# Attention products of a fused block as four products on 128x32 blocks of the TensorE array

## The chip, the cores and the metric

The kernel runs on one core of a Trainium2 chip. The metric is device time in microseconds, from the start of the program on the core to its end; the median of several runs is given. The profile is of one execution. PE is the matmul engine (TensorE), PEld its weight loads, DVE is VectorE, ACT is ScalarE, POOL is GpSimd and SP is the engine that issues most DMAs.

## The reference

An adaLN transformer block on x of shape (4, 2048, 256): batch 4, 2048 tokens, 256 channels. The attention has 16 heads of 16 channels, the second half of which is rotated by position.

```
h = layernorm(x) * (1 + ca) + sa
q, k, v = up-projections of h @ Wq_down, h @ Wk_down, h @ Wv_down      # 16 heads of 16
scores = q @ k.T / 4, causal mask, softmax over the keys
x = x + ga * ((att @ v) @ Wc)
h = layernorm(x) * (1 + cb) + sb
x = x + gb * moe(h)              # top 2 of 12: 8 experts of 512 hidden units, 4 that pass h on
```

## The kernel before, in words

`project` (from L254) normalises x, forms q, k and v by fp32 products on the whole 128x128 array and writes them out. q and k are split in three bf16 parts each, and six pairs of parts (L49) are stacked on the partitions, so that one bf16 product of 96 rows sums them. `attention` (from L827) follows; `route` and `experts` come after it and are not touched.

**Iterations.** The attention runs 16 times (NIT, L45): four batches by four groups of four heads. Every loop is unrolled. One iteration has two halves, and the halves of successive iterations overlap.

*Maxima.* For each tile of 128 queries and each chunk of up to 512 keys, PE multiplies queries by keys into PSUM, and DVE takes the maximum over the keys. The work is cut into 73 units (`UNITS`, L201 to L206) of two or four heads. `unit_products` (L221) issues one product of 96 rows, 128 columns of queries as weights and w keys as the moving operand, per head (L227); on the diagonal one more product per head adds the mask by way of the identity (L231). `unit_maxima` (L239) is DVE's reduction. Two PSUM buffers of two banks serve the units (NRED, L207): PE waits on `red_done` before it refills one. The first 13 units of iteration 0 are issued at the end of `project` (L677 to L680).

*The turn.* Four times per iteration DVE forms the negated maxima of 512 queries, POOL splits them in three bf16 parts (L1061), and PE turns these 48 columns into 48 rows (`turn`, L1131); DVE copies them out, and SP writes them as three more rows under the queries (L951).

*Scores, exponentials, values.* For each of 40 tiles of 128 keys by up to 512 queries (`KT`, L843), PE multiplies keys by queries once more, now with 99 rows, so that the maximum is subtracted in the product (`scores`, L1144), ACT takes the exponential from PSUM (L1192, three PSUM banks), POOL zeroes the upper triangle on diagonal tiles (L1077), and PE multiplies the values by the result (`values`, L1160). A value product is fp32, has 32 columns of weights per head, and the four heads of a tile go to four 32-partition blocks of one PSUM bank. One fp32 product is recorded as two matmuls, so a tile is a group of eight. Every other product of the attention has 128 columns of weights, the turn 48.

**The order.** `Course` (L683) is a planner that runs when the kernel is built. From costs in microseconds per operation (L686 to L688) it lays out the order in which PE takes units, turns, scores and values; POOL's and SP's orders and DVE's stream come from the same plan. A unit may run ahead of the scores by a fixed share (RUN_AHEAD). ENTER (0.09) and LEAVE (0.147) are the costs that it counts when a group of value products begins after, or is followed by, another kind of work (L717, L765, L771). Each engine then runs its list in order, and waits on semaphores.

Of the kernel before, what the change touches and what calls it, by code (L numbers as in the profile page):

```python
# [30 lines left out]
P = 128  # L31
# [12 lines left out]
NG = H // HG  # L44
NIT = B * NG  # L45
SLOT = 32
QB = 256
NJ = T // QB
COMBOS = [(0, 0), (0, 1), (1, 0), (1, 1), (0, 2), (2, 0)]  # L49
SROWS = 16 * len(COMBOS)  # L50
MROWS = 3
# [27 lines left out]
def apart(eng):  # L79

    eng.nop(nofuse=True)
# [51 lines left out]
def build(nc, a, out):  # L133
    d, retired = {}, []
    with ExitStack() as ctx:
        def dram(name, shape, dt):
            d[name] = nc.dram_tensor(name, shape, dt, kind="Internal").ap()

        dram("q_parts", (3, B, H, DH, T), BF16)
        dram("k_parts", (3, B, H, DH, T), BF16)  # L140
        dram("v_ones", (B, NG, P, TT, HG * SLOT), F32)
        dram("attn_t", (B, NG, P, T), F32)
# [69 lines left out]
def unit_view(ps, u, at):  # L212

    _, _, _, nh, w = UNITS[u]
    buf = ps[:, 4:8, :].rearrange("p (u n) w -> p u n w", u=NRED)[:, at % NRED, :, :]
    if w > 256:
        return buf[:, :, 0:w]
    return buf.rearrange("p n w -> p (n w)")[:, 0:nh * w].rearrange("p (h w) -> p h w", h=nh)


def unit_products(pe, k, ps, ks, qs, u, at):  # L221

    i, c, h0, nh, w = UNITS[u]
    o, diag = unit_view(ps, u, at), c == i // 4
    for h in range(nh):
        first = w > 256 or h % (512 // w) == 0
        ins = pe.matmul(o[:, h, :], qs[0:SROWS, h0 + h, i * P:(i + 1) * P], ks[0:SROWS, h0 + h, 512 * c:512 * c + w],  # L227
                        start=first, stop=not diag, skip_group_check=w <= 256)
    if diag:
        for h in range(nh):  # L230
            ins = pe.matmul(o[:, h, w - P:w], k["identb"][:, :], k["mask_qk"][:, :],  # L231
                            start=False, stop=True, skip_group_check=w <= 256)
    return ins


# [18 lines left out]
def project(nc, a, d, k, ps, g0, retired):  # L254
    with ExitStack() as ctx:
        def sb(name, shape, dt=F32):
            return ctx.enter_context(nc.sbuf_tensor(name, shape, dt))
# [15 lines left out]
        parts = sb("parts", [P, 2, 3, 2, NM, BLK], BF16)  # L273
        vout = sb("vout", [P, 2, TPB, H, SLOT])
        tab_ld, norm_step, std_done, hn_done, tr_done, ht_done, ones_done = (
# [36 lines left out]
        with nc.Block() as block:  # L312
# [265 lines left out]
            def _(pe):  # L578
# [98 lines left out]
                for u in range(HEAD):  # L677
                    if u >= NRED:
                        pe.wait_ge(g0["red_done"], u - NRED + 1)
                    unit_products(pe, k, ps, g0["ks"], g0["qs"], u, u).then_inc(g0["red_ready"], 1)  # L680


class Course:  # L683


    MM, MUL, MASK, ENTER, LEAVE, LATE, HOP = 1 / 2400, 0.0045, 0.0565, 0.09, 0.147, 0.1, 0.2  # L686
    TURN_PE, TURN_DVE, ROWS, ROWS_LATER, SPLIT, AFFINE, OUT, QUARTER_MAX, LOAD = 0.12, 0.3, 6.0, 10.0, 1.6, 0.65, 0.58, 0.2, 8.0
    SCALE, RUN_AHEAD, PREFER_DVE = 1.3, 0.16, 0.3  # L688

# [137 lines left out]
def attention(nc, a, d, k, ps, g0, first, retired):  # L827
    with ExitStack() as ctx:
        def sb(name, shape, dt=F32):
            return ctx.enter_context(nc.sbuf_tensor(name, shape, dt))  # L830
# [8 lines left out]
        QJ = 512  # L839
# [24 lines left out]
        for n in range(NIT):  # L864
            now, rest = [], []
            for x in ([1, 2] if n == 0 else [n + 2]):
                if x < NIT:
                    rows = [(what, x, m) for m in range(len(COMBOS)) for what in ("ks", "qs")]
# [19 lines left out]
        QUARTER = HG * KPJ  # L888
# [3 lines left out]
        ks = [g0["ks"], lent[0], sb("ks2", [P, HG, T], BF16)]  # L892
        qs = [g0["qs"], lent[1], sb("qs2", [P, HG, T], BF16)]
        num, x_in = routed_inputs(k)
        vs = sb("vs", [P, R, TT, HG * SLOT])
        probs = sb("probs", [P, NPB, HG, QJ])
# [5 lines left out]
        mparts = sb("mparts", [P, NJ, HG, MROWS, KPJ], BF16)  # L902
# [5 lines left out]
        red_ready, red_done = g0["red_ready"], g0["red_done"]  # L908
# [13 lines left out]
        def st_view(n, s):  # L922

            m, _, nh = SETS[s]
            w = QJ - KT[m][2]
            return st_ps[:, (NSET * n + s) % NST, 0:nh * w].rearrange("p (h w) -> p h w", h=nh)

        with nc.Block() as block:
            @block.sync
            def _(sp):  # L930
# [22 lines left out]
                def denominators(n):  # L953

                    for r in range(2):
                        sp.wait_ge(o_st[r], 16 * NJ // 2 * (n + 1) + 1)
                    rows = d["attn_t"][n // NG, n % NG].rearrange("(h s) (c t) -> h s c t", s=SLOT, t=HG * T // P)
                    sp.dma_start(den[:, :], rows[:, DH, :, :]).then_inc(den_ld, 16)
# [26 lines left out]
                def outputs(n, half):  # L985

                    rows = d["attn_t"][n // NG, n % NG].rearrange("(h s) t -> s h t", s=SLOT)
                    return rows[0:DH, :, half * SC:(half + 1) * SC]
# [125 lines left out]
            @block.tensor  # L1114
            def _(pe):
                def group(n, u, at):

                    r = n % R
                    if u == 0:
                        pe.wait_ge(ld[r], LD * (n // R + 1))  # L1120
                    if at >= NRED:
                        pe.wait_ge(red_done, at - NRED + 1)
                    unit_products(pe, k, ps, ks[r], qs[r], u, at).then_inc(red_ready, 1)

                def turn(n, q, at):

                    pe.wait_ge(part_step, PART * (NJ * n + q + 1))
                    pe.wait_ge(red_done, at - NRED + 1)
                    apart(pe)
                    o = red_ps[0:MROWS * QUARTER, at % NRED, 0, :].bitcast(BF16)  # L1130
                    pe.transpose(o[:, 0:P], mparts[:, q, :, :, :].rearrange("p h m i -> p (h m i)"), k["identb"][:, :]).then_inc(red_ready, 1)  # L1131

                def scores(n, r, s):

                    m, h0, nh = SETS[s]
                    J, j, lo = KT[m]
                    o = st_view(r, s)
                    if s == 0 and 0 < n < R:
                        pe.wait_ge(ones_ld, 16 * (R - 1))
                    if h0 == 0 and j == 0:  # L1140
                        pe.wait_ge(m_ld, M_LD * (NJ * n + J + 1) + 1)
                    pe.wait_ge(exp_done, NSET * n + s + 1)
                    for h in range(nh):
                        ins = pe.matmul(o[:, h, :], ks[r][0:SROWS + MROWS, h0 + h, j * P:(j + 1) * P],  # L1144
                                        qs[r][0:SROWS + MROWS, h0 + h, J * QJ + lo:(J + 1) * QJ], start=True, stop=True)
                    ins.then_inc(st_ready, 1)

                def values(n, r, m):

                    J, j, lo = KT[m]  # L1150
                    if m == 0:
                        pe.wait_ge(v_ld[r], 16 * NV * (n // R + 1))
                    if j == 0:
                        pe.wait_ge(o_done, NJ * n + J + 2)
                    if m in DIAG:
                        pe.wait_ge(mask_done, len(DIAG) * n + DIAG.index(m) + 1)
                    else:
                        pe.wait_ge(exp_done, NSET * n + of_tile[m][-1] + 1 + NST)
                    for g in range(HG):
                        ins = pe.matmul(o_ps[SLOT * g:SLOT * (g + 1), lo:QJ], vs[:, r, j, SLOT * g:SLOT * (g + 1)],  # L1160
                                        probs[:, (NKT * r + m) % NPB, g, 0:QJ - lo], start=(j == 0), stop=(m == LAST[J]))
                    ins.then_inc(pv_done, 1)

                for kind, n, x in course.pe_order:
                    if kind == "scores":
                        scores(n, n % R, x)
                    elif kind == "values":
                        values(n, n % R, x)
                    elif kind == "turn":
                        turn(n, x, unit_at[n, TURN + x])  # L1170
                    elif n > 0 or x >= HEAD:
                        group(n, x, unit_at[n, x])
                pe.wait_ge(wc_done, B)
                pe.wait_ge(first["o"][0], 16 * KC)
                pe.wait_ge(red_done, len(course.stream))
                apart(pe)
                projected(pe, k, projected_bank(ps, 0), num, 0).then_inc(first["out"][0], 1)
# [231 lines left out]
def routed_inputs(k):  # L1409

    return (k["shared"][:, 0, :].rearrange("p (x k b) -> p x k b", x=XB, k=KC),
            k["shared"][:, 1, :].rearrange("p (x j c) -> p x j c", x=XB, j=TPB))
# [9 lines left out]
def projected_bank(ps, j):  # L1422

    return ps[:, 4 + 2 * j:6 + 2 * j, :].rearrange("p n (j c) -> p (n j) c", j=2)


def projected(pe, k, o, num, t):

    for n in range(TPB):
        for c in range(KC):  # L1430
            ins = pe.matmul(o[:, n, :], num[:, t % XB, c, n * P:(n + 1) * P], k["wc"][:, t // BPS, c, :],
                            start=(c == 0), stop=(c == KC - 1))
    return ins
# [695 lines left out]
```

## Time and profile before

| | |
|---|---|
| median of 3 runs | 2607.42 us |
| lowest and highest | 2605.97 and 2611.03 us |
| span of the profiled execution, first to last instruction | 2600.7 us |
| the median less this span | 6.7 us |
| mean granted TensorE clock over the span | 0.970 of 2.4 GHz |
| busy: PE, DVE, ACT, POOL | 95%, 73%, 64%, 29% |
| matmuls and weight loads | 16056 and 16057 |

The profile gives no time of its own for the execution beside its span; the 6.7 us are what lies before the first and after the last instruction, as far as one execution can be set against the median of others. A row of a timeline reads: start, length, engine, line, operation, output<-inputs, form of the operands (weights' rows\*columns, then rows x moving columns and type), and the number of instructions merged in it; its length reaches from the start of the first to the end of the last. The starts are measured, the ends of matmuls are modelled. An idle time behind a row is the engine's own before it.

### The profile page before, as it was taken

The page shows a single profiled execution, that of the slowest core. Times are in us where ns is not written, and L with a number is a line of the kernel's source. Part 1 is how long each engine was busy: PE and PEld are TensorE (multiplying, and loading weights), DVE is VectorE, ACT ScalarE, POOL GpSimd, SP SyncE. Part 2 cuts the span into 40 slices and gives each one's busy share as a digit, 9 for nine tenths or more (in the row PEclk, how much of TensorE's full clock was granted, in tenths as well). Part 3 has the DMA queues.
Part 4 walks back from the last instruction along what each step waited for, and adds up shares of the span by engine and source line. Part 5 has one row for each costly group of instructions (what it writes and reads, how often), then busy time and mean ns, then how long its engine had stood idle before and what let it go on. Part 6 is the DMA issues. An engine that isn't in the chain of part 4 may idle for free. (4 is left out here: it accounts for less than half of the span.)

```text
span 2600.7 us, 47842 instructions
## 1 busy us (share of the span) xinstructions
PE 2470.6 (95%) x16056; PEld 1274.6 (49%) x16057; DVE 1905.6 (73%) x3219; ACT 1670.9 (64%) x2983; POOL 765.4 (29%) x894
## 2 busy tenths in 40 slices
PE   6987789999999999999999999999999889999998
PEld 3554223333333333333333333333327779899897
DVE  5887778888787887887877878878836854455665
ACT  1656347777777777777777777777775455555554
POOL 2545311111111111211111111111112657677554
PEclk8999689999999999999999999999999889999999
DMA  5698653252432433434424323231027656575665
GB/s 181 198 255 217 136 86 88 66 116 79 96 92 75 93 86 86 86 83 92 91 78 100 88 73 78 64 73 39 27 82 215 214 185 131 105 136 114 104 104 84
DMA packets 224510, 285.59 MB, mean 110 GB/s; under 512 B 29462, under 2 KB 177974, under 8 KB 223926
## 3 DMA queue, kind: packets, MB, share of 16 engines
q1 hardware_dynamic: 185308, 235.53, 35.9%
q0 software_dynamic: 31872, 41.30, 9.4%
q10 hardware_dynamic: 7136, 6.32, 0.8%
q8 instruction: 103, 1.69, 0.3%
q14 instruction: 91, 0.75, 0.1%
HBM read 143.37 MB, written 138.81 MB: 109 GB/s over the span
## 5 line engine op out<-in xcount | busy, mean ns | idle before, releaser
L239 DVE TENSOR_REDUCE mxc<-ps 128x2 f32<-128x1024 f32 (+4 forms) x1168 | 1297.7, 1149 | 314.9 <-PE ps L227 165.9
L1192 ACT ACTIVATE probs<-ps 128x512 f32<-128x512 f32 (+1 forms) x2240 | 1177.9, 587 | 461.0 <-PE ps L1144 449.2
L1160 PE MATMUL ps<-probs,vs 128*32 128x512 f32 (+3 forms) x5120 | 601.3, 542 | 1.2 <-POOL probs L1077 1.2
L1144 PE MATMUL ps<-qs,ks 99*128 99x512 bf16 (+3 forms) x1760 | 505.0, 353 | 10.6 <-DMA qs<-m_t 6.6
L227 PE MATMUL ps<-ks,qs 96*128 96x512 bf16 (+3 forms) x1760 | 465.1, 355 | 27.7 <-DVE mxc L239 18.0
L1077 POOL TENSOR_SCALAR_AFFINE_SELECT probs<-probs 128x512 f32<-128x512 f32 x256 | 162.0, 636 | 870.8 <-ACT probs L1192 870.7
L1144 PEld LDWEIGHTS ps<-qs,ks 99*128 99x128 bf16 x1760 | 147.9, 97 | 379.0 <-ACT probs L1192 270.3
L227 PEld LDWEIGHTS ps<-ks,qs 96*128 96x128 bf16 x1760 | 163.6, 99 | 181.5 <-DVE mxc L239 42.7
L1921 PE MATMUL ps<-x_t,w_at 128*128 128x128 f32 x1968 | 243.0, 277 | 0.0
L2052 POOL DMA_INDIRECT out<-ys,idx x120 | 192.6, 1605 | 138.4 <-DMA out<-ys,idx 85.1
L1921 PEld LDWEIGHTS ps<-x_t,w_at 128*128 128x128 f32 x1968 | 232.7, 194 | 0.2 <-ACT w_at L1966 0.2
L1144 PE MATMUL ps<-shared 99*128 99x512 bf16 (+3 forms) x800 | 228.4, 349 | 0.0
L1930 PE MATMUL ps<-w2t,hid_t 128*128 x960 | 227.2, 379 | 0.0
L1160 PEld LDWEIGHTS ps<-probs,vs 128*32 128x32 f32 x5120 | 101.0, 108 | 228.9 <-issue 119.1
L227 PE MATMUL ps<-shared 96*128 96x512 bf16 (+3 forms) x800 | 206.8, 348 | 2.0 <-DVE mxc L239 1.8
L1930 PEld LDWEIGHTS ps<-w2t,hid_t 128*128 128x128 f32 x960 | 173.2, 190 | 18.7
L2021 DVE TENSOR_TENSOR ys<-ps,gm 128x256 f32<-128x256 f32 x120 | 50.9, 425 | 177.4 <-PE ps L1930 127.4
L1966 ACT COPY w_at<-shared 128x1024 f32 x126 | 131.8, 1046 | 56.7 <-issue 53.7
L1962 ACT COPY x_t<-ps 128x256 f32<-128x256 f32 x126 | 46.9, 372 | 160.5 <-PE ps L1913 157.2
L1061 POOL CAST mparts<-negm 128x16 bf16<-128x16 f32 x64 | 12.6, 197 | 461.4 <-DVE negm L1211 461.4
L1382 POOL DMA_INDIRECT slot_x<-h,pos x128 | 130.6, 1020 | 59.4 <-issue 35.0
L1144 PEld LDWEIGHTS ps<-shared 99*128 99x128 bf16 x800 | 66.9, 96 | 163.7 <-ACT probs L1192 118.2
(175 smaller groups left out, 2217.6 us busy)
## 6 DMA issues: line engine op xcount, KB each, us to landing
ks<-k_parts SPq DMA_DIRECT2D x66, 256.0 KB, 4.1
qs<-q_parts SPq DMA_DIRECT2D x66, 256.0 KB, 4.1
xs<-slot_x SPq DMA_DIRECT2D x126, 131.0 KB
v_ones<-vout SPq DMA_DIRECT2D x64, 256.0 KB, 3.7
vs<-v_ones SPq DMA_DIRECT2D x64, 256.0 KB, 3.2
attn_t<-o_sb SPq DMA_DIRECT2D x64, 256.0 KB, 3.1
slot_x<-zero SPq DMA_DIRECT2D x48, 262.0 KB, 2.6
q_parts<-parts SPq DMA_DIRECT2D x96, 128.0 KB, 2.5
```

The source lines that it names most:

```text
L227: ins = pe.matmul(o[:, h, :], qs[0:SROWS, h0 + h, i * P:(i + 1) * P], ks[0:SROWS, h0 + h, 512 * c:512 * c + w], start=first, stop=not diag ...
L239: return dve.tensor_reduce(mxc[:, h0:h0 + nh, i, c], unit_view(ps, u, at), AX_X, ALU.max)
L1077: pool.affine_select(at, at, pattern=[[0, HG], [1, P]], base=0, channel_multiplier=-1, compare_op=ALU.is_ge, fill=keep).then_inc(mask_done, 1)
L1144: ins = pe.matmul(o[:, h, :], ks[r][0:SROWS + MROWS, h0 + h, j * P:(j + 1) * P], qs[r][0:SROWS + MROWS, h0 + h, J * QJ + lo:(J + 1) * QJ], ...
L1160: ins = pe.matmul(o_ps[SLOT * g:SLOT * (g + 1), lo:QJ], vs[:, r, j, SLOT * g:SLOT * (g + 1)], probs[:, (NKT * r + m) % NPB, g, 0:QJ - lo], ...
L1192: act.activation(probs[:, (NKT * r + m) % NPB, h0:h0 + nh, 0:QJ - lo], st_view(r, s), ACT.Exp, scale=DH ** -0.5).then_inc(exp_done, 1)
L1382: pool.indirect_dma_start(d[f"slot_x{p}"][:, :], bass.IndirectOffsetOnAxis(ap=r["pos"][c][:, t:t + 1], axis=0), r["h2"][:, t, :], None).th ...
L1921: ins = pe.matmul(ph[:, q, f * P:(f + 1) * P], w1_at[:, q, c, f * P:(f + 1) * P], x_t[:, q, c, :], start=(c == 0), stop=(c == KC - 1))
L1930: ins = pe.matmul(py[:, q, 0:C], h_t[:, q, f, :], w["w2t"][:, bass.ds(e, 1), f, :].rearrange("p o c -> p (o c)"), start=(f == 0), stop=(f ...
L1966: act.copy(w1_at[:, q, :, :], w["w1t"][:, bass.ds(e, 1), :, :].rearrange("p o c f -> p (o c) f")).then_inc(w1_done[p], 1)
L2021: dve.tensor_tensor(ys[:, t % YR, :], py[:, q, 0:C], gm[:, t % YR, :], ALU.mult).then_inc(y_done[p], 1)
L2052: pool.indirect_dma_start(rows, bass.IndirectOffsetOnAxis(ap=idx[:, p, t:t + 1], axis=0), ys[:, t % YR, :], None, compute_op=ALU.add).then ...
```

## The change

All attention products that had 128 columns of weights are issued as four products of 32 columns, one per 32-partition block of the output. `QUADS` holds the four slices. In `unit_products` each product and each mask product becomes four, with the same moving operand; on the diagonal every one of the four keeps all of its moving columns (up to 512 for the scores, 128 for the mask). `scores` does the same. The turn's transpose of 48 columns becomes two, of 32 and 16. The semaphore is raised by the last product only, as before. In the planner ENTER and LEAVE are set to 0, so that the order of PE's work, and with it those of POOL, SP and DVE, is laid out anew. The data, the sums and the buffers stay as they are.

```diff
--- before.py
+++ after.py
@@ -44,6 +44,7 @@
 NG = H // HG
 NIT = B * NG
 SLOT = 32
+QUADS = [slice(q * SLOT, (q + 1) * SLOT) for q in range(P // SLOT)]
 QB = 256
 NJ = T // QB
 COMBOS = [(0, 0), (0, 1), (1, 0), (1, 1), (0, 2), (2, 0)]
@@ -224,12 +225,14 @@
     o, diag = unit_view(ps, u, at), c == i // 4
     for h in range(nh):
         first = w > 256 or h % (512 // w) == 0
-        ins = pe.matmul(o[:, h, :], qs[0:SROWS, h0 + h, i * P:(i + 1) * P], ks[0:SROWS, h0 + h, 512 * c:512 * c + w],
-                        start=first, stop=not diag, skip_group_check=w <= 256)
+        for at_q in QUADS:
+            ins = pe.matmul(o[at_q, h, :], qs[0:SROWS, h0 + h, i * P + at_q.start:i * P + at_q.stop],
+                            ks[0:SROWS, h0 + h, 512 * c:512 * c + w], start=first, stop=not diag, skip_group_check=w <= 256)
     if diag:
         for h in range(nh):
-            ins = pe.matmul(o[:, h, w - P:w], k["identb"][:, :], k["mask_qk"][:, :],
-                            start=False, stop=True, skip_group_check=w <= 256)
+            for at_q in QUADS:
+                ins = pe.matmul(o[at_q, h, w - P:w], k["identb"][:, at_q], k["mask_qk"][:, :],
+                                start=False, stop=True, skip_group_check=w <= 256)
     return ins
 
 
@@ -683,7 +686,7 @@
 class Course:
 
 
-    MM, MUL, MASK, ENTER, LEAVE, LATE, HOP = 1 / 2400, 0.0045, 0.0565, 0.09, 0.147, 0.1, 0.2
+    MM, MUL, MASK, ENTER, LEAVE, LATE, HOP = 1 / 2400, 0.0045, 0.0565, 0.0, 0.0, 0.1, 0.2
     TURN_PE, TURN_DVE, ROWS, ROWS_LATER, SPLIT, AFFINE, OUT, QUARTER_MAX, LOAD = 0.12, 0.3, 6.0, 10.0, 1.6, 0.65, 0.58, 0.2, 8.0
     SCALE, RUN_AHEAD, PREFER_DVE = 1.3, 0.16, 0.3
 
@@ -1128,7 +1131,11 @@
                     pe.wait_ge(red_done, at - NRED + 1)
                     apart(pe)
                     o = red_ps[0:MROWS * QUARTER, at % NRED, 0, :].bitcast(BF16)
-                    pe.transpose(o[:, 0:P], mparts[:, q, :, :, :].rearrange("p h m i -> p (h m i)"), k["identb"][:, :]).then_inc(red_ready, 1)
+                    rows = mparts[:, q, :, :, :].rearrange("p h m i -> p (h m i)")
+                    for lo in range(0, MROWS * QUARTER, SLOT):
+                        part = slice(lo, min(lo + SLOT, MROWS * QUARTER))
+                        ins = pe.transpose(o[part, 0:P], rows[:, part], k["identb"][:, :])
+                    ins.then_inc(red_ready, 1)
 
                 def scores(n, r, s):
 
@@ -1141,8 +1148,9 @@
                         pe.wait_ge(m_ld, M_LD * (NJ * n + J + 1) + 1)
                     pe.wait_ge(exp_done, NSET * n + s + 1)
                     for h in range(nh):
-                        ins = pe.matmul(o[:, h, :], ks[r][0:SROWS + MROWS, h0 + h, j * P:(j + 1) * P],
-                                        qs[r][0:SROWS + MROWS, h0 + h, J * QJ + lo:(J + 1) * QJ], start=True, stop=True)
+                        for at_q in QUADS:
+                            ins = pe.matmul(o[at_q, h, :], ks[r][0:SROWS + MROWS, h0 + h, j * P + at_q.start:j * P + at_q.stop],
+                                            qs[r][0:SROWS + MROWS, h0 + h, J * QJ + lo:(J + 1) * QJ], start=True, stop=True)
                     ins.then_inc(st_ready, 1)
 
                 def values(n, r, m):
```

## Rows read from the trace of the kernel before

**Rows 1.** The page: busy time, share of the span and instructions of each engine.

```profile
PE 2470.6 (95%) x16056; PEld 1274.6 (49%) x16057; DVE 1905.6 (73%) x3219; ACT 1670.9 (64%) x2983; POOL 765.4 (29%) x894
```

**Rows 2.** An iteration in tenths: busy us (instructions) by engine, PEclk, DMA share, GB/s.

```profile
1279.48:1289.74 10.26, 10.26 (x72) 3.65 (x69) 9.19 (x9) 7.99 (x16) 1.91 (x2) 1.00 1.02 170
1289.74:1300.01 10.27, 10.27 (x74) 3.80 (x73) 7.28 (x9) 7.38 (x14) 2.07 (x5) 1.00 0.31 61
...
sum 102.63, PE 102.47 PEld 37.31 DVE 82.95 ACT 75.29 POOL 15.79; mean PE 10.25 PEld 3.73 DVE 8.29 ACT 7.53 POOL 1.58
```

**Rows 3.** Waits 500 to 1900 us; over the span; a group, 400 to 1900 us.

```profile
ACT probs L1192 <- PE ps L1144: 363.1, 545, 1.5
...
DVE mxc L239 <- PE ps L227: 133.2, 275, 1.3
...
PE ps L227 <- DVE mxc L239: 19.9, 18, 12.2
...
L227 PE MATMUL ps<-ks,qs 96*128 96x512 bf16 (+3 forms) x1582 | 407.6, 347 | 0.3 <-DVE mxc L239 0.3
```

**Rows 4.** PE (and its weight loads, PEld) in order of time at 1200 us; durations of L1160.

```profile
1200.43 0.38 PE L1144 MATMUL ps<-qs,ks 99*128 99x512 bf16 x1
1200.74 1.06 PE L1160 MATMUL ps<-probs,vs 128*32 128x512 f32 x8
1201.74 0.39 PE L1144 MATMUL ps<-qs,ks 99*128 99x512 bf16 x1
1201.96 0.60 PE L227 MATMUL ps<-ks,qs 96*128 96x512 bf16 x2
...
1200.74 0.16 PEld L1160 LDWEIGHTS ps<-probs,vs 128*32 128x32 f32 x8 [0.27 <-ACT probs L1192]
...
L1160 PEld LDWEIGHTS ps<-probs,vs x8: 106/108/109, 1200.7 to 1200.8; 128*32 128x32 f32 x8
L1160 PE MATMUL ps<-probs,vs x8: 592/604/617, 1200.7 to 1201.2; 128*32 128x512 f32 x8
```

**Rows 5.** The same view around the turn at 1207.64 us.

```profile
1206.64 1.06 PE L1160 MATMUL ps<-probs,vs 128*32 128x512 f32 x8
1207.64 0.24 PE L1131 MATMUL ps<-identb,mparts 128*48 128x128 bf16 x1
1207.81 0.40 PE L1144 MATMUL ps<-qs,ks 99*128 99x128 bf16 x4
```

**Rows 6.** Groups of PE's instructions over the span, with their counts.

```profile
L1160 PE MATMUL ps<-probs,vs 128*32 128x512 f32 (+3 forms) x5120 | 601.3, 542 | 1.2 <-POOL probs L1077 1.2
L1144 PE MATMUL ps<-qs,ks 99*128 99x512 bf16 (+3 forms) x1760 | 505.0, 353 | 10.6 <-DMA qs<-m_t 6.6 <-ACT probs L1192 3.4
L227 PE MATMUL ps<-ks,qs 96*128 96x512 bf16 (+3 forms) x1760 | 465.1, 355 | 27.7 <-DVE mxc L239 18.0 <-PEq L312 4.8 <-ACT vout L554 4.1
...
L1144 PE MATMUL ps<-shared 99*128 99x512 bf16 (+3 forms) x800 | 228.4, 349 | 0.0
...
L227 PE MATMUL ps<-shared 96*128 96x512 bf16 (+3 forms) x800 | 206.8, 348 | 2.0 <-DVE mxc L239 1.8
...
L231 PE MATMUL ps<-mask_qk,identb 128*128 128x128 bf16 x1024 | 125.2, 222 | 0.0
```

**Rows 7.** PE in order of time, L629 at 16 us and L1160 at 305 us.

```profile
15.99 1.07 PE L629 MATMUL ps<-parts,up 128*32 128x256 f32 x16
...
304.95 1.28 PE L1160 MATMUL ps<-probs,vs 128*32 128x384 f32 x16
```

**Rows 8.** PE's sequencer waits at L607 and L626 (start in us), and the densest 5 us.

```profile
L607 PEldq EVENT_SEMAPHORE  x1: 51/51/51, 18.1 to 18.1; - x1
...
L626 PEldq EVENT_SEMAPHORE  x1: 51/51/51, 18.4 to 18.4; - x1
...
372.98:377.98 5.00, 5.00 (x60) 2.40 (x57) 4.25 (x6) 1.39 (x3) 2.06 (x6) 1.00 0.71 129
```

**Rows 9.** The page: the larger instruction queue, its packets, MB and share of 16 engines.

```profile
q8 instruction: 103, 1.69, 0.3%
```

## The prediction

> **What bounds the kernel now.** I read the page's busy times first [rows 1]: TensorE (PE) 95% of the span, VectorE (DVE) 73%, ScalarE (ACT) 64%. A busy share over stages of different kinds says little, so next I cut one attention iteration, from one first turn to the next, into ten stretches [rows 2]. The reader is to see that the iteration lasts 102.63 us, that PE is busy 102.47 of it at a granted clock of 1.00 (the 2.4 GHz level) in every tenth (two of them stand in the rows), that DVE works 82.95 us and ACT 75.29 us, and that in no tenth is either busier than PE. There are 16 such iterations, so the attention block is about 1640 of 2600.7 us. The waits say the same [rows 3]: DVE and ACT wait for PE's products hundreds of times, and PE for DVE, between 400 and 1900 us, 0.3 us in all. PE is the bound here; a microsecond taken off its work is worth up to a microsecond, until DVE (82.95 us per iteration) is in the way.
>
> But busy PE need not be streaming. The order of PE's instructions in time shows where it is not [rows 4]. A 512-wide bf16 product starts 0.22 us before the next (1201.74 to 1201.96), which is 512 columns at 2.4 GHz, 0.213, and little else. Ahead of a value group it is 0.31 (1200.43 to 1200.74): 0.09 more. The value group streams two passes of 512 columns at half a column per cycle, 2 x 0.427 = 0.853, yet the next score product starts 1.00 after it: 0.14 more. So one trip from 128x128 blocks to 128x32 blocks and back costs 0.23 us of a busy-looking PE. The turn (L1131), which has 48 columns, shows the same [rows 5]: it follows a value group, and 0.17 passes from its start to the next product, where 128-column products stand 0.06 apart; where it follows a score product it also pays the 0.09.
>
> **What the change removes.** 5120 value instructions are 640 groups of eight, 40 per iteration [rows 6]. 40 x 0.23 = 9.2 us per iteration. Four turns at 0.09 + 0.11 = 0.8, less 0.2 because two or three of the four adjoin a value group and share a crossing with it. Together 9.8 us per iteration, 157 us over 16. Without them PE has 102.6 - 9.8 = 92.8 us of work.
>
> **What it adds.** Per iteration 160 score products, 160 unit products and 64 masks (2560, 2560 and 1024 over 16) [rows 6] become four each on neighbouring blocks: 384 batches of four, 6144 in all, 18432 new matmuls and as many weight loads. The question is what a batch takes. No row shows four bf16 streams; the fp32 ones are nearest. Their weight loads start 0.007 us apart (eight in 0.16, each 0.108 long) [rows 4], so the fourth block runs 0.02 behind the first. The first pass of a group needs 0.45 to the second (group 1.06 long, last product 0.59, so its start is 0.47 after the first, less 0.02) where its columns need 0.427: 0.025 over. Is that paid by every batch, or only after a crossing? [Rows 7] decide it for fp32. Four passes of 256 columns (L629) have their last start 1.07 - 0.38 = 0.69 after the first; less 0.02 and the dear first pass (0.238), two more passes took 0.216 each: the bare columns, 0.213. Two value groups back to back at 304.95 give the same: last start 0.90 after the first, of which 0.88 is 0.345 + 0.320 + 0.213. So once the array is in 128x32 blocks, a batch costs what its columns cost, like one 128x128 product today. I take **nothing** for a batch. Below nothing is excluded: the columns are the same. The upper end: for 256, 384 and 512 columns the fp32 rows cover the same lengths of time; the 128-column ones (four diagonal tiles by four heads are 16 scores and 16 units, and 64 masks, per iteration) last 0.056 now (0.053 of columns and the 0.003 of any product; four in a row at 1207.81 give (0.40 - 0.224)/3 = 0.059 with rounded starts [rows 5]), and the shortest pass on four blocks is that of 128 columns of fp32, 2 x 0.053 = 0.107. If they need that, 96 x 0.051 = 4.9 us per iteration, 78 us in all.
>
> The turn becomes two transposes of 32 and 16 columns, side by side: nothing. Each semaphore comes 0.02 later, from the fourth block; 73 units and 140 sets per iteration wait on such, but most start behind work of their own engine: nothing while PE is ahead, and part of the waits below when it is not. Sequencer: 8 instructions in place of 2. Two wait instructions with 32 PE instructions of the weight turns between them (L607, L626) run 18.1 and 18.4 in [rows 8], about 0.01 us each; a 128-column batch has 8 in 0.056, a 512-column one 8 in 0.216. Nothing, with that narrow margin. Instruction fetch: the larger of the two queues moves 103 packets, 1.69 MB, in 0.3% of the DMA engines' time [rows 9]; two or three times that stays under 1%.
>
> ENTER and LEAVE at 0 make the planner lay another order on PE, and from it on POOL and SP. POOL works 15.79 us of the iteration [rows 2]; I cost the reorder at nothing as long as the order follows the true costs, which it then does.
>
> **What comes in place of the crossings.** If PE needs 92.8 us, DVE must be busy 82.95/92.8 = 89% of the time, with two PSUM buffers between them, while a value group holds PE 0.87 us. Today it is 81% and PE never waits. The fullest tenth has DVE at 9.19/10.26 = 90% with PE full [rows 2], so 89% isn't impossible, but it is reached in one tenth out of ten, the lowest stands at 71%. Bounds: 92.8 us (no wait) and 102.6 (all waits). I take DVE at the middle, 85%: 82.95/0.85 = 97.6 us, a gain of 5.0 us in each of 15 steady iterations; the first is ruled by waits for DVE and loads (before L227, 19.9 us over the whole span but 0.3 between 400 and 1900 us [rows 3]), so I give it none. **75 us.** Sum: the profiled span is 2600.7, so 2526 there; the runs' median 2607.4 lies 6.7 above that span, which the change leaves alone: **2532 us**.
>
> **Rivals.**
> A: the short batches are dear. Floor 92.8 + 4.9 = 97.7; half of what is left to 102.6 lost in waits, 100.2: gain 2.4 x 15 = 36, 2571 us. For: no row has a 0.056 batch. Against: nothing shows a limit either.
> B: no waits come back: 2607 - 157 = 2450. For: the 90% tenth. Against: nine others.
> C, the slower side: the 0.025 of a first pass is the loading of weights that nobody hid, and bf16 batches, each with its own four loads behind a semaphore, pay it every time. 384 x 0.025 = 9.6, PE at 102.4 per iteration; with 0.02 of later release in perhaps 50 exposed waits, 1.0 more: 103.4, so +0.8 x 16 = 13, 2620 us. It decides from about 75/6144 = 0.012 us per batch. Against: [rows 7]. The Trainium skill, TensorEngine Tiling (Array Packing), section Restrictions, says column tiling turns fast weight load off, which would speak for C if loads don't hide: by that rule the time is C's, 2620, against 2532 by [rows 7]. No row here shows a bf16 load on a 32-column block.
> D: PE's sequencer can't feed four times the instructions. 1864 matmuls and as many loads per iteration are 3728; the densest 5 us shows 117 in 5.00, 0.043 each [rows 8]. Were that the limit, 160 us per iteration, 3530 us. Against: the 18.1 and 18.4 of [rows 8]; nothing shows that 0.043 was the sequencer's doing. The Trainium skill, TensorE: Matmul & The Clock Gate, section "Wait — 56ns, not 53.3ns?", gives 62 ns per matmul where the sequencer decodes in its own code; an estimate by that page is 116 us per iteration and some 2820 us. The same price range holds if four bf16 streams don't run at once.
> E: it does nothing: the waits of DVE and ACT take back all 9.8: 2605.
>
> **How the numbers follow.** Forecast 0.56 (its own range 2495 to 2575), A 0.10, B 0.08, C 0.14, D 0.09, E 0.03. Two tenths of a percent, 5 us, is about what a measurement tells from no change. Faster: forecast, A, B and a sliver of C, 0.75; same: E and C's middle, 0.04; slower: the rest of C and D, 0.21. The range leaves out D and most of B: 2465 to 2620.
>
> **What would show it.** After, an iteration near 97 us (turn to turn); score to value 0.216 instead of 0.31; value to score 0.86 instead of 1.00; starts of 512-wide batches still 0.216 apart (C: 0.24) and of mask batches 0.056 (A: about 0.11); DVE busy near 85% in the steady stretch; PE with gaps ended by DVE and ACT. Batches at 0.4 would be D and make the prediction wrong outright; PE busy 99% and 102 us again would be C.

## The result and the profile after

| | before | after |
|---|---|---|
| median (lowest, highest), us | 2606.7 (2603.6, 2611.0), 4 runs | 2527.4 (2524.1, 2529.8), 4 runs |
| ratio after to before, 95% interval | | 0.970 [0.9684, 0.9717] |
| span of the profiled execution, us | 2600.7 | 2522.3 |
| one attention iteration, mean of the last 15 (fourth turn to fourth turn), us | 102.5 | 98.0 |
| PE work in one iteration without waits, as the prediction reckons it, us | 102.6 | 92.8 |

The kernel is 3.0% faster; the forecast was 2532 us. From the page of the changed kernel: the busy line and the larger instruction queue (packets, MB, share of the DMA engines).

```profile
PE 2355.7 (93%) x34552; PEld 1479.6 (59%) x34553; DVE 1902.3 (75%) x3219; ACT 1660.3 (66%) x2983; POOL 766.7 (30%) x894
...
q8 instruction: 247, 4.05, 0.8%
```

Against [rows 1] and [rows 9]: PE has 18496 more matmuls and is busy 115 us less, DVE and ACT do the same work as before, and instruction fetch went from 103 packets to 247.

The crossings are gone. PE in order of time, start and length in us, as in [rows 4]:

```profile
1200.48 0.44 PE L1152 MATMUL ps<-qs,ks 99*32 99x512 bf16 x4
1200.70 1.08 PE L1168 MATMUL ps<-probs,vs 128*32 128x512 f32 x8
1201.56 0.44 PE L1152 MATMUL ps<-qs,ks 99*32 99x512 bf16 x4
1201.78 0.66 PE L229 MATMUL ps<-ks,qs 96*32 96x256 bf16 x16
```

The value group now starts 0.22 us after the score batch (0.31 before), and the next score batch 0.86 after the value group (1.00 before). The batch of four at 1201.56 holds the array until 1201.78, 0.22 us, as one product of 128 columns did. The one surprise in these rows is the length 0.44 of four products of 0.38 each: the four blocks do not start 0.007 apart but are spread over 0.06. Each keeps its own pace: single records of the batch at 1200.48 start at 1200.482, .483, .519 and .538, and each block's next product starts 0.22 later.

What did not come is the rest of the 9.8 us per iteration. One iteration of the changed kernel, its first tenth, its last and the whole, with the columns of [rows 2]:

```profile
1270.64:1280.46 9.82, 9.40 (x162) 4.53 (x166) 7.65 (x9) 6.79 (x13) 0.00 (x0) 0.83 0.10 33
1359.04:1368.86 9.82, 8.19 (x206) 4.82 (x198) 8.28 (x10) 3.91 (x8) 3.37 (x8) 1.00 0.47 110
1270.64:1368.86 98.22, 95.87 (x1866) 50.83 (x1866) 82.84 (x83) 74.64 (x144) 15.95 (x34) 0.98 0.41 93
```

DVE works 82.84 of 98.22 us, 84%; the prediction had taken 85%. But the missing time is not spread over the iteration. In the last tenth ACT works 3.91 us of 9.82 and PE stands idle 1.6, and in the first tenth of the iteration, right behind the same place of the one before, the granted clock is 0.83. The timeline there shows a hole; first PE, then ACT (idle before the row in brackets, with what ended it):

```profile
1362.70 0.43 PE L1152 MATMUL ps<-shared 99*32 99x128 bf16 x16
...
1365.53 0.43 PE L1168 MATMUL ps<-probs,vs 128*32 128x128 f32 x8
1366.15 0.62 PE L229 MATMUL ps<-ks,qs 96*32 96x512 bf16 x8 [0.19 <-DVE mxc L242]
1367.66 0.41 PE L229 MATMUL ps<-ks,qs 96*32 96x128 bf16 x16 [0.90 <-DVE mxc L242]
1367.90 0.40 PE L234 MATMUL ps<-mask_qk,identb 128*32 128x128 bf16 x16
1368.84 0.23 PE L1137 MATMUL ps<-identb,mparts 128*32 128x128 bf16 x2 [0.55 <-issue]
1369.39 0.62 PE L229 MATMUL ps<-ks,qs 96*32 96x512 bf16 x8 [0.33 <-DVE mxc L242]
1369.83 0.82 PE L1152 MATMUL ps<-shared 99*32 99x512 bf16 x12
```

```profile
1363.25 0.60 ACT L1200 ACTIVATE probs<-ps 128x512 f32<-128x512 f32 x1 [0.56 <-PE ps L1152]
1370.34 1.09 ACT L1200 ACTIVATE probs<-ps 128x512 f32<-128x512 f32 x2 [6.49 <-PE ps L1152]
```

From 1362.7 to 1369.8 PE gets no score product. It has finished the scores up to query 1536; the next ones, for the last 512 queries, need the rows of the turn that ran at 1358.77. In between the order has only units, the values of finished tiles and one more turn. With two buffers the units wait for reductions of DVE, and PE stands idle 0.19 + 0.90 + 0.55 + 0.33 us; DVE ends three of these waits, and for the 0.55 before the turn the profile names nothing. The hole is there once in every iteration: between 450 and 1750 us ACT has 14 idle stretches of over 2 us, 91.5 us together, 13 of them this hole; the trace of before has one, of 3.9 us. At 8 of the 13 holes the granted clock falls to half for 3.4 or 6.8 us; before, it never fell in that stretch. The window rows agree: 98.22 at a mean clock of 0.98.

The mask row also settles the short batches: four batches of 128 columns (x16) take 0.40 in all, 0.22 of it the last product's own length; the other three take 0.18, about 0.06 each.

### The profile page after: what moved, and what is told of

The parts are those of the page before. It is cut to its first block and busy times, and to the rows that moved or that the text cites. A ratio compares the mean times of both kernels' runs of the same rounds, so it can differ in the third digit from the quotient of the medians.

```text
span 2522.3 us, 84848 instructions
## 1 busy us (share of the span) xinstructions
PE 2355.7 (93%) x34552; PEld 1479.6 (59%) x34553; DVE 1902.3 (75%) x3219; ACT 1660.3 (66%) x2983; POOL 766.7 (30%) x894
## 5 line engine op out<-in xcount | busy, mean ns | idle before, releaser
L1168 PE MATMUL ps<-probs,vs 128*32 128x512 f32 (+3 forms) x5120 | 588.8, 529 | 3.1 <-ACT probs L1200 1.7
L229 PE MATMUL ps<-ks,qs 96*32 96x512 bf16 (+3 forms) x7040 | 495.8, 360 | 48.8 <-DVE mxc L242 35.3
L1152 PE MATMUL ps<-qs,ks 99*32 99x512 bf16 (+3 forms) x7040 | 534.4, 356 | 7.0 <-ACT probs L1200 3.1
L229 PEld LDWEIGHTS ps<-ks,qs 96*32 96x32 bf16 x7040 | 197.6, 99 | 242.9 <-DVE mxc L242 85.8
L1152 PEld LDWEIGHTS ps<-qs,ks 99*32 99x32 bf16 x7040 | 200.2, 97 | 237.3 <-ACT probs L1200 101.7
L1152 PE MATMUL ps<-shared 99*32 99x512 bf16 (+3 forms) x3200 | 237.7, 349 | 0.2
L229 PE MATMUL ps<-shared 96*32 96x512 bf16 (+3 forms) x3200 | 219.6, 353 | 9.9 <-DVE mxc L242 9.8
L1168 PEld LDWEIGHTS ps<-probs,vs 128*32 128x32 f32 x5120 | 168.2, 110 | 91.6 <-ACT o_sb L1192 10.7
L1152 PEld LDWEIGHTS ps<-shared 99*32 99x32 bf16 x3200 | 89.6, 95 | 99.9 <-ACT probs L1200 39.0
```

The source lines that it names most:

```text
L229: ins = pe.matmul(o[at_q, h, :], qs[0:SROWS, h0 + h, i * P + at_q.start:i * P + at_q.stop], ks[0:SROWS, h0 + h, 512 * c:512 * c + w], star ...
L1152: ins = pe.matmul(o[at_q, h, :], ks[r][0:SROWS + MROWS, h0 + h, j * P + at_q.start:j * P + at_q.stop], qs[r][0:SROWS + MROWS, h0 + h, J * ...
```

## The experiments

The theory from these rows (W): the crossings are the gain; what is missing, 98.0 against 92.8 us per iteration, are waits that the order makes. Rivals: the new order and not the block shape is the gain (R); each batch of four costs 0.014 us more than its columns (B). Each ratio is to the kernel before as it ran beside that set of runs (2606, 2615 and 2612 us for the labels in a, b and c); runs of different sets are compared by ratio or by iteration.

### The order and the products apart

The changed products with the planner's old numbers:

```diff
-    MM, MUL, MASK, ENTER, LEAVE, LATE, HOP = 1 / 2400, 0.0045, 0.0565, 0.0, 0.0, 0.1, 0.2
+    MM, MUL, MASK, ENTER, LEAVE, LATE, HOP = 1 / 2400, 0.0045, 0.0565, 0.09, 0.147, 0.1, 0.2
```

> The change's products with the planner's old ENTER and LEAVE (0.09, 0.147), so the order of before. Theory W (the crossings between block shapes are the gain, and what is missing from it, 98.0 us per iteration where PE has 92.8 of work, are waits that the order makes): the crossings are gone all the same, so most of the gain stays: 2505 to 2545 us. Rival R (the gain comes from the new order, and the products are only neutral): 2590 us or more. Rival B (each batch of four costs 0.014 us more than its columns, 384 x 0.014 = 5.2 us per iteration): 2527, as the changed kernel.

Measured: 2467.5 us, ratio to before 0.9469 [0.9453, 0.9485]; an iteration takes 93.9 us. That is 60 us **faster** than the changed kernel and outside all that was expected. R and B both fall: the products earn 139 us without the new order, and the same batches of four run in 93.9 us per iteration. Of W, the first half stands and the second is stronger than stated: with the old order most of the 9.8 us come (8.6 of them).

And the products of before in the new order, the same line the other way round:

> The products of before with ENTER and LEAVE at 0, so the new order alone. Theory W: every crossing is paid, PE has 102.6 us per iteration and some waits besides: 2605 to 2640 us. Rival R: 2530 to 2560 us.

Measured: 2663.3 us, ratio 1.0216 [1.0199, 1.0233], 106.9 us per iteration. R is out, and W's range (up to 2640) was too low as well: the order costs more than either theory had it. The hole is in this trace too (ACT idle 6.5 to 7.1 us once per iteration), although PE still pays every crossing. The new order by itself costs 4.4 us per iteration with the old products and 4.1 with the new ones: the two parts of the change add up, one worth -139 us and one +57 to +60.

One iteration with the new products in the old order, and the waits of ACT, DVE and PE from 500 to 1750 us there (us in total, times, longest):

```profile
1230.97:1324.70 93.73, 93.17 (x1870) 48.44 (x1866) 82.69 (x83) 75.50 (x144) 15.90 (x35) 1.00 0.41 97
```

```profile
ACT probs L1200 <- PE ps L1152: 233.5, 481, 1.6
DVE mxc L242 <- PE ps L229: 70.2, 177, 0.8
...
PE ps L1137 <- issue: 7.2, 13, 0.6
```

and in the changed kernel, the same view and stretch:

```profile
ACT probs L1200 <- PE ps L1152: 276.1, 430, 7.1
DVE mxc L242 <- PE ps L229: 118.4, 244, 2.7
...
PE ps L229 <- DVE mxc L242: 19.8, 49, 0.9
```

With the old order DVE is busy 88% (82.69 of 93.73) and PE never waits for it; ACT's longest wait is 1.6 us, not 7.1. The 88% that the prediction thought hard to reach are reached in a steady stretch. In the new order PE waits longest for DVE, and some 17 of the 19.8 us lie in the hole.

The cost of the new order can be split. Eleven iterations of the changed kernel, and eleven of the one with the old order:

```profile
572.52:1652.64 1080.12, 1052.02 (x20519) 553.67 (x20510) 909.68 (x902) 820.65 (x1584) 175.44 (x374) 0.99 0.39 90
565.28:1597.25 1031.97, 1025.46 (x20519) 526.11 (x20511) 909.54 (x902) 830.61 (x1584) 174.91 (x375) 1.00 0.40 94
```

An iteration is 4.4 us longer (98.2 against 93.8). Idle time of PE is 2.0 of that (28.1 against 6.5 us in eleven). The clock stands at half for 30.7 us in the first row and never in the second; half of that time lost is an estimate of 1.4 us per iteration. The lengths of iterations agree: from 680 us on, four of the five without a fall take 96.7 or 96.8 us, those with a fall of 3.4 us 98.2 to 98.7. The last 1.0 us is shown as busy. Most of it is probably waiting too, since a 512-wide product is drawn 0.38 us long and holds the array for 0.22, so that a wait behind it shows 0.16 short; that split isn't shown. So less than half of the cost is idle time that the profile shows as such, and a third is the lower clock behind it.

### Less work for DVE

The unit's reduction reads half of its columns, so half of the maxima's work is left out:

```diff
-    i, c, h0, nh, _ = UNITS[u]
-    return dve.tensor_reduce(mxc[:, h0:h0 + nh, i, c], unit_view(ps, u, at), AX_X, ALU.max)
+    i, c, h0, nh, w = UNITS[u]
+    return dve.tensor_reduce(mxc[:, h0:h0 + nh, i, c], unit_view(ps, u, at)[:, :, 0:w // 2], AX_X, ALU.max)
```

> The changed kernel, but DVE's reduction reads only the first half of each unit's columns, so half of the maxima's work is left out; the order is the same. Theory W: PE no longer waits for DVE, an iteration falls from 98.0 to 93 or 94 us: 2455 to 2475 us. Rival B: the batches themselves are dear, an iteration stays at 97 or more: 2510 to 2527 us.

Measured: 2472.7 us, ratio 0.9484 [0.9468, 0.9499], 94.35 us in most iterations. The waits of the changed kernel were for DVE, as W says: PE's idle time between 450 and 1750 us falls from 35.3 to 11.7 us. ACT's hole stays, though, at 4.9 us per iteration in place of 6.5 to 7.1, and no longer costs PE much: the clock falls once between 450 and 1750 us, not 8 times. Taking half of the load off DVE gains no more than the old order does with all of it on.

### Where the hole comes from

Two of the planner's numbers act on it. ROWS_LATER is its estimate of the time from a turn's copy to its rows under the queries; in the trace they land 4.1 us after the first of the four DMAs is issued (median of 64 turns, read from the DMA records), and the planner reckons 10. In the hole shown above the first of the four is issued at 1360.43, so the rows are there at about 1364.5, some 5 us before PE takes the first score product that needs them. PREFER_DVE, where it is positive, puts scores ahead of units.

```diff
-    TURN_PE, ..., ROWS_LATER, ... = 0.12, ..., 10.0, ...
-    SCALE, RUN_AHEAD, PREFER_DVE = 1.3, 0.16, 0.3
+    TURN_PE, ..., ROWS_LATER, ... = 0.12, ..., 8.0, ...
+    SCALE, RUN_AHEAD, PREFER_DVE = 1.3, 0.16, -0.3
```

> The changed kernel with two numbers of the planner changed: ROWS_LATER 8 in place of 10 (the rows of maxima land 4.1 us after the first issue in the trace), PREFER_DVE -0.3 in place of 0.3 (units are taken earlier). Theory W: once per iteration, before the scores of the last 512 queries, ACT idles 6.5 to 7.1 us and PE 2.2 us, because the units have fallen behind and the order puts the scores behind them; with units earlier this goes, and an iteration falls from 98.0 to about 95 us: 2475 to 2500 us. Rival B (dear batches): 2520 to 2530 us.

Measured: 2473.9 us, ratio 0.9454 [0.9436, 0.9472], 93.7 us per iteration, a little better than W's range. ACT has one idle stretch of over 2 us left (2.4 us), PE 5.1 us of idle time in place of 35.3, and the clock no longer falls there. It was run again beside the last three kernels.

> ROWS_LATER 8 and PREFER_DVE -0.3 once more, on the chip of the three others: a ratio to before of 0.945 again, 2465 to 2478 us; theory O says this and the kernel with PREFER_DVE alone differ by the remnant of the hole, 10 to 20 us, rival O2 by 40 us and more.

Measured: 2472.5 us, ratio 0.9460 [0.9444, 0.9476]: the same.

ROWS_LATER at 8 alone:

> The changed kernel with ROWS_LATER 8 in place of 10 alone. Theory W: the scores of the last 512 queries are put some 2 us earlier, the wait of ACT and PE before them shortens, about 1.0 to 1.5 us per iteration: 2502 to 2515 us. Rival B: 2525 to 2530 us.

Measured: 2504.6 us, ratio 0.9578 [0.9562, 0.9594], 96.0 us per iteration. Two microseconds less in the estimate shorten ACT's hole by nearly two. ACT in that run:

```profile
1348.07 4.43 ACT L1200 ACTIVATE probs<-ps 128x512 f32<-128x512 f32 x8 [4.78 <-PE ps L1152]
```

PREFER_DVE at -0.3 alone:

> The changed kernel with PREFER_DVE -0.3 in place of 0.3, ROWS_LATER left at 10. Theory O (since the two runs on the order: the 60 us between 2527 and 2467 are one hole per iteration before the scores of the last 512 queries, because scores are preferred and the units fall behind): with units preferred the hole closes without touching ROWS_LATER: 94 to 95 us per iteration, 2475 to 2495 us. Rival O2 (the hole comes from the 10 us that the planner counts for the rows, and only that): 2515 to 2530 us.

Measured: 2488.1 us, ratio 0.9521 [0.9505, 0.9537], 94.6 us per iteration: theory O. With units preferred, the turn for the last 512 queries comes early enough and the hole is gone although the planner still reckons 10 us. Two numbers make the hole, and they weigh differently: the preference for scores, by which the units fall behind, closes it alone, and the 10 us, by which the scores are held back longer than the DMAs take, close part of it alone. The two changes together are another 0.9 us per iteration better than the preference alone (15.6 us in all, within the 10 to 20 that O gave). A third mix, to look for the floor:

> The changed kernel with the planner's MUL 0.0025, ENTER 0.03, LEAVE 0.048, ROWS_LATER 4.5 and PREFER_DVE 0.04, to see whether an order can do better than the two of 2467 and 2474 us. Theory O: PE's work of 92.8 us per iteration is the floor and those two stand at 93.8 and 93.5, so at most 10 us are left: 2460 to 2480 us.

Measured: 2478.0 us, ratio 0.9486 [0.9469, 0.9503], 94.0 us per iteration. No better; three different orders end at 93.7 to 94.0 us, against 92.8 of reckoned work. In all three PE is busy 93.2 to 93.5 us per iteration and idle 0.3 to 0.6, so little is left for an order to gain. The best two kernels are the changed products in the old order (0.9469) and with units preferred and rows at 8 (0.9454 and 0.9460); their intervals overlap, and both beat before and after.

### The price of a crossing

The turn as one transpose of 48 columns again:

```diff
-                    for lo in range(0, MROWS * QUARTER, SLOT):
-                        part = slice(lo, min(lo + SLOT, MROWS * QUARTER))
-                        ins = pe.transpose(o[part, 0:P], rows[:, part], k["identb"][:, :])
+                    ins = pe.transpose(o[:, 0:P], rows, k["identb"][:, :])
```

> The changed kernel with the turn as one transpose of 48 columns again: four crossings there and back per iteration. If they are paid: 4 x 0.20 = 0.8 us per iteration, 13 us, 2540 us. If they hide in the wait that PE has at the turn anyway (0.55 us at one turn of four): 2527 to 2537 us.

Measured: 2539.2 us, ratio 0.9738 [0.9719, 0.9756], 98.8 us per iteration: 0.8 us more with four crossings there and back, as the first expectation has it. Not all of that need be crossings: over eleven iterations PE's busy time grows by 0.9 us each, of which an estimated 0.3 is the lower clock (at half for 37.6 us, against 30.7), and its idle time shrinks by 0.2. (Its interval and the changed kernel's touch, from 0.9684 to 0.9717 and from 0.9719; the iteration's length is the firmer sign.)

The mask on the whole array again:

```diff
-            for at_q in QUADS:
-                ins = pe.matmul(o[at_q, h, w - P:w], k["identb"][:, at_q], k["mask_qk"][:, :],
-                                start=False, stop=True, skip_group_check=w <= 256)
+            ins = pe.matmul(o[:, h, w - P:w], k["identb"][:, :], k["mask_qk"][:, :],
+                            start=False, stop=True, skip_group_check=w <= 256)
```

> The changed kernel with the mask products on the whole array again. 25 units per iteration lie on the diagonal, each now pays a crossing there and back of 0.21 to 0.23 us: 5.2 to 5.8 us per iteration. If PE pays them beside its waits: +80 to +90 us, 2607 to 2617 us. If they partly take the place of waits for DVE (PE has 98.0 - 92.8 = 5.2 us of those): +40 to +60 us, 2567 to 2587 us.

Measured: 2600.5 us, ratio 0.9943 [0.9922, 0.9965], 102.4 us per iteration. Its PE, in order of time:

```profile
1201.12 0.62 PE L229 MATMUL ps<-ks,qs 96*32 96x512 bf16 x8
1201.67 0.28 PE L233 MATMUL ps<-mask_qk,identb 128*128 128x128 bf16 x2
1201.88 0.62 PE L229 MATMUL ps<-ks,qs 96*32 96x512 bf16 x8
```

Two batches take 0.55 in place of 0.43, and two masks 0.21 in place of 0.11: 0.22 us for the trip. 25 trips are 5.5 us; 4.4 were measured, since some of them took the place of waits: over eleven iterations PE's busy time without the estimated price of the clock grows by 5.2 us each, its idle time shrinks by 0.7 and the price of the clock by 0.3. By the ratios the kernel is 63 us slower than the changed one, just between the two expectations (40 to 60 and 80 to 90). One kind of product left at 128 columns takes back four fifths of what the change brings (0.9943 against 0.970).

### How near the limit of issue is

Each unit product cut into pieces of 128 moving columns, the same columns in all:

```diff
-            ins = pe.matmul(o[at_q, h, :], qs[...], ks[0:SROWS, h0 + h, 512 * c:512 * c + w],
-                            start=first, stop=not diag, skip_group_check=w <= 256)
+            for x in range(0, w, P):
+                ins = pe.matmul(o[at_q, h, x:x + P], qs[...], ks[0:SROWS, h0 + h, 512 * c + x:512 * c + x + P],
+                                start=first and x == 0, stop=not diag and (w <= 256 or x + P == w), skip_group_check=w <= 256)
```

> The changed kernel with each unit product cut into pieces of 128 moving columns: the same columns, 1536 more matmuls and as many weight loads per iteration, 6800 PE instructions in 98 us, 0.0144 us each. If PE's sequencer and its instruction fetch have reserve: 384 more pieces in a row per block at 0.003 = 1.2 us per iteration, 2527 to 2550 us. If the change stood near a limit of issue (rival D of the prediction): 2650 us or more.

Measured: 2771.2 us, ratio 1.0593 [1.0573, 1.0612], 113.1 us per iteration. There is a limit, and it is not far. PE's waits from 500 to 1750 us and the instruction queue of that run:

```profile
PE ps L230 <- issue: 65.5, 71, 4.3
PE ps L1154 <- issue: 18.2, 15, 3.3
PE ps L1170 <- issue: 17.1, 10, 3.9
```

```profile
q8 instruction: 439, 7.19, 1.2%
```

"issue" means that the engine waited for nothing that the profile shows. The 192 packets more are 49152 instructions more (16 x 3072), 256 per packet, so the queue feeds PE. In the DMA records the beginnings of such packets can be set beside the ends of PE's waits. All 44 idle stretches of over 1 us in the steady part that "issue" ends are over 2.5 to 3.4 us after the beginning of a packet (one of 4.29 us ended at 596.2; the packet began at 593.0 and took 1.32). Over the whole span no two packets begin less than 3.3 us apart; in the changed kernel none come closer than 4.3 us. Per iteration PE is idle 11.2 us (2.6 in the changed kernel), and the clock at half costs an estimated 2.9 us more. In pieces of 256 columns, in the old order:

> The changed products in the old order (2467 us), each unit product cut into pieces of at most 256 moving columns: 512 more matmuls and as many weight loads per iteration, 4752 PE instructions in 94 us. With pieces of 128 (6800 instructions) the kernel took 2771 us, and PE stood idle up to 4.5 us at a time right behind a packet of the instruction queue. Theory F (fetch: a packet of 256 instructions comes no sooner than 3.4 us after the last, so dense runs starve; at 8 instructions per 0.109 us a packet lasts 3.5 us): hardly any such idle time, 2467 to 2490 us. Rival S (each further instruction costs PE's sequencer the same, (2771 - 2527)/16/3072 = 0.005 us): 1024 x 0.005 = 5.1 us per iteration, 2540 to 2555 us.

Measured: 2524.1 us, ratio 0.9656 [0.964, 0.9672], 96.4 us per iteration against 93.9. Neither expectation: by the ratios it is 49 us slower than the kernel with whole units (0.9656 against 0.9469), where F had at most 23 and S 73 to 88. PE's waits, same stretch:

```profile
PE ps L231 <- issue: 15.0, 12, 2.6
PE ps L1140 <- issue: 6.4, 12, 0.5
PE ps L1155 <- issue: 2.1, 3, 1.1
```

PE starves here too, 12 times in 1250 us before a unit, about once per iteration; the nine idle stretches of over 1 us that "issue" ends are over 2.8 to 3.4 us after the beginning of a packet, and here too no two packets begin less than 3.3 us apart. (The waits of about 0.5 us before one turn per iteration are in the kernel with whole units as well, so they aren't this.) That the time is lost while a packet is on its way is shown for both kernels; that fetch and not some other limit behind it sets the 3.3 us is an inference. Over eleven iterations this kernel is 2.8 us per iteration slower than the one with whole units: 1.7 of it is idle time of PE, 0.3 an estimate for two falls of the clock, and 0.8 stays open.

## Why the prediction was right, and where it was not

- **The bound and the crossings.** Right. 9.8 us per iteration were reckoned; with the order held still the products bring 8.6. The 1.1 us between the 93.9 and the reckoned 92.8 are in two halves: PE is idle 0.6 us, and its busy time is 93.2 and not 92.8. Taking back the turn alone cost 0.8 for four trips, the masks alone 0.22 per trip in the rows.
- **A batch costs its columns.** Right, also for 128 columns (mask batches start 0.057 apart, the median of 291 units in the changed kernel's steady stretch) and for bf16 (0.217 for 512 columns). The fp32 passes of [rows 7] were the right rows to judge by. Rivals A and C fall with it: neither short batches nor hidden loads cost anything. The Trainium skill, TensorEngine Tiling (Array Packing), section Restrictions, rules fast weight load out on column tiles. No run here shows whether it was off; the loads of 32 bf16 columns are drawn 0.096 us long and are hidden behind batches 0.057 us apart, so the rule changes nothing in this kernel.
- **The blocks 0.02 us behind one another.** Too small at times, up to 0.06, and without a price that shows: mask batches stay 0.057 apart.
- **Sequencer and fetch cost nothing.** Right for this change, for a poor reason. The share of the DMA engines' time was the wrong number; what counts is how soon a packet of 256 instructions can follow the last. Rival D named the issue limit and priced it where it isn't, at 0.043 us per instruction: the changed kernel runs at 98.0/3728 = 0.026 on average. But it is real, and twice the instructions in the units meet it. The Trainium skill, TensorE: Matmul & The Clock Gate, section "Wait — 56ns, not 53.3ns?", gives 62 ns per matmul where the sequencer decodes by its own code; 1864 matmuls in 93.9 us, 0.050 each, rule that case out here.
- **The reorder at nothing "as long as the order follows the true costs, which it then does".** Wrong. This is the step that failed: it costs 57 to 60 us. The order follows the true costs of the crossings better, and yet is worse, because another number of the planner (10 us for rows that land in 4.1) and its preference for scores now make the units fall behind and leave a hole. Both did no such harm while ENTER and LEAVE were counted. It is the planner's account that matters and not PE's real speed: the old products in the new order have the same hole.
- **Waits take back half, 5.0 of 9.8 gained per iteration.** The number was right (4.5 gained, DVE at 84%), its reason wrong. It was taken from friction between DVE and PE with two buffers, spread over the iteration. There is next to none of that: DVE runs at 88% in the old order with PE never waiting for it. Nearly the whole loss comes with the hole, part of it by way of the clock, which the prediction had left at 1.00. So two mistakes met: a reorder that was priced at 0 and cost 60, and waits that were priced at 157 - 75 = 82 and in the old order are 157 - 139 = 18, some 6 of which are PE's extra busy time. That 2532 came so close to 2527 is luck.
- **The first iteration gains nothing.** Right: the last of its turns comes at 377 us in both traces. The 15 iterations gained 67 us; the stretch from the last turn to the end of the attention gained 9, which the prediction didn't count, and the rest of the kernel 2, together the 78 by which the spans differ.
- **Rival B, 2450 us**, was closer to what the change could do (2467) than the forecast; it had 0.08.

## What to carry to other kernels

A mix of block shapes on TensorE costs 0.2 us per trip and looks like busy time; if most work fits one shape, put all of it in that shape, down to the smallest product. When an order is written by a planner, a change of its costs is a change of its own: test products and order apart, since here one was worth -139 us and the other +60, and the changed kernel shows only their sum. Look for a loss in time and not in shares: an average of 84% for DVE fitted a wrong story, the timeline showed one hole per iteration.

## What the runs showed of the hardware

- Four 128x32 blocks with four bf16 streams run fully side by side at the 2.4 GHz level, at 512 columns (0.217 us) as at 128 (0.057), and mostly start within 0.06 us of one another, each block at its own pace.
- Weight loads of 32 bf16 columns are hidden behind batches 0.057 us apart.
- PE's instructions come in packets of 256. At 6800 instructions per iteration PE starved, up to 4.3 us at a time, and packets kept at least 3.3 us apart, 0.013 us per instruction; at 4752 it still starved about once per iteration; at 3728 in the old order it had no such wait before a unit, a score or a value product.
- Short idle times of PE can cost twice: at 8 of 13 holes with some 2 us of PE idle, the granted clock was at half (1.2 GHz) for 3.4 or 6.8 us, and an iteration with a fall of 3.4 us took about 1.5 us longer. With the hole closed it stayed at 1.00 through the steady stretch.
